# Second attention of a two-layer model: scores turned before the exponential, mask and maximum added in PSUM, division left to the last mixture

## What is computed

```python
h = h + _L1_attn_ref(_layernorm(h, axis=-1), L1_attn_Wq, L1_attn_Wk, L1_attn_Wv, L1_attn_Wo)
h = h + _L1_ffn_ref(_layernorm(h, axis=-1), L1_ffn_A, L1_ffn_B, L1_ffn_Wr, L1_ffn_br)
...
draft = jnp.einsum('bhqd,bhkd->bhqk', qr, kr)
draft = draft + jnp.where(causal_future, neg, jnp.asarray(0.0, dtype))
_, draft_indices = jax.lax.top_k(draft, num_remain)     # num_remain = 128
mask = mask.at[b_idx, h_idx, s_idx, draft_indices].set(0.0)   # all else: neg
scores = jnp.einsum('bhqd,bhkd->bhqk', qr, kr) / np.sqrt(HD).astype(np.float32) + mask
attn = jax.nn.softmax(scores, axis=-1)
out = jnp.einsum('bhqk,bhkd->bhqd', attn, v)
```

## Time and profile before

| | us |
|---|---|
| median of 3 runs (5139.87 to 5142.20) | 5141.41 |
| the profiled execution, its own time | 5140.53 |
| its span in the trace | 5138.70 |
| PE busy | 3749.4 (73%) |
| DVE busy | 3507.8 (68%) |
| ACT busy | 3167.7 (62%) |

### The profile page before, as it was taken

How to read it: one execution, slowest core, us unless ns; L and a number is a source line. 1 busy time by engine, 2 the same in 40 slices (tenths; PEclk the granted TensorE clock), 3 DMA queues, 4 the chain that set the end, 5 groups by cost and what they waited for, 6 DMA issues and landing times. The chain is left out here.

```text
span 5138.7 us, 79699 instructions
## 1 busy us (share of the span) xinstructions
PE 3749.4 (73%) x23338; PEld 2207.5 (43%) x23480; DVE 3507.8 (68%) x10383; ACT 3167.7 (62%) x7058; POOL 289.1 (6%) x213
## 2 busy tenths in 40 slices
PE   6998999999999999924555355555555555554799
PEld 2445766666444444412333233333333333332454
DVE  3564777776333356558888888888888888887444
ACT  1123777776000011169999599999999999999200
POOL 2332000000000023300000000000000000000000
PEclk8999999999999999966766676666766767766899
DMA  4235323232111123310011011111011110110222
GB/s 150 64 70 157 78 54 79 57 76 94 57 49 49 49 49 76 77 37 10 17 27 26 1 26 26 26 23 25 6 26 26 24 25 6 24 26 6 79 86 78
DMA packets 276875, 249.81 MB, mean 49 GB/s; under 512 B 170048, under 2 KB 209232, under 8 KB 276432
## 3 DMA queue, kind: packets, MB, share of 16 engines
q1 hardware_dynamic: 275888, 245.13, 18.1%
q0 software_dynamic: 544, 0.07, 0.0%
HBM read 167.56 MB, written 77.59 MB: 48 GB/s over the span
## 5 line engine op out<-in xcount | busy, mean ns | idle before, releaser
L1036 ACT ACTIVATE a_sign<-a_x,a_state 128x384 fp8e4<-128x384 f32 (+5 forms) x1536 | 1343.0, 876 | 124.4 <-DVE a_state L1172 85.7
L942 PE MATMUL a_ps_s<-k,q 128*128 128x512 bf16 (+3 forms) x1474 | 500.1, 484 | 689.5 <-DVE a_x L1273 660.0
L953 PE MATMUL a_ps_t<-ident,arena 128*128 128x128 f32 x2304 | 484.8, 355 | 193.9 <-ACT a_invT L1005 130.1
L942 PEld LDWEIGHTS a_ps_s<-k,q 128*128 128x128 bf16 x1536 | 167.4, 130 | 914.6 <-DVE a_x L1273 748.3
L971 PE MATMUL a_ps_o<-a_probT,vals 128*32 128x128 f32 x4608 | 407.4, 327 | 184.8 <-ACT a_probT L1001 184.4
L953 PEld LDWEIGHTS a_ps_t<-ident,arena 128*128 128x128 f32 x2304 | 338.4, 179 | 332.8 <-ACT a_invT L1005 142.9
L727 ACT ACTIVATE a_prob<-a_x_neg,a_shift 128x640 f32<-128x640 f32 (+7 forms) x512 | 397.1, 776 | 79.4 <-DVE a_x_neg L770 61.2
L1273 DVE TENSOR_SCALAR_CACHE_REDUCE a_x<-a_ps_s 128x128 f32<-128x128 f32 (+7 forms) x512 | 383.7, 754 | 85.4 <-PE a_ps_s L945 60.4
L1001 ACT COPY a_probT<-a_ps_t 128x512 f32<-128x512 f32 (+3 forms) x768 | 346.6, 476 | 111.1 <-PE a_ps_t L953 110.1
L770 DVE TENSOR_SCALAR_CACHE_REDUCE a_x_neg<-a_ps_s 128x640 f32<-128x640 f32 (+7 forms) x512 | 378.8, 751 | 38.4 <-PE a_ps_s L651 25.4
L971 PEld LDWEIGHTS a_ps_o<-a_probT,vals 128*32 128x32 f32 x4608 | 269.2, 128 | 294.4 <-ACT a_probT L1001 268.2
(11 more groups left out here) (229 smaller groups left out, 5941.4 us busy)
## 6 DMA issues: line engine op xcount, KB each, us to landing
q<-qk SPq DMA_DIRECT2D x256, 256.0 KB, 4.8
qk<-p_qkT SPq DMA_DIRECT2D x32, 960.0 KB, 6.2
h_rows<-h SPq DMA_DIRECT2D x32, 512.0 KB, 6.9
k<-qk SPq DMA_DIRECT2D x256, 64.0 KB, 5.1
h<-tok_h SPq DMA_DIRECT2D x16, 512.0 KB, 4.0
arena<-in_wo SPq DMA_DIRECT2D x16, 512.0 KB, 9.0
o<-a_o SPq DMA_DIRECT2D x16, 512.0 KB, 2.7
q<-o SPq DMA_DIRECT2D x16, 512.0 KB, 5.6
```

What stands on the lines that cost most here:

```text
L942: nc.tensor.matmul(ps_s[:, n % 2, a:a + w], q[:, y, head, i * P:(i + 1) * P], k[:, y, a:a + w], start=(y == 0), stop=False, skip_group_che ...
L953: mm = nc.tensor.transpose(ps_t[:, (n + 1) % 3, c:c + P], prob[:, par, at:at + P], ident[:, :])
L1036: ins = nc.scalar.activation(to, x[:, par, at:at + w], ACT.Sign, scale=-1.0, saturate=False, bias=state[:, par, 0, n:n + 1], accum_out=sta ...
```

## The change

In the second attention:
- The exponentials on ACT (16 a pair) are gone, and so is `keep`. DVE instead writes a mask for each of the 14 tiles, `mark`: 0 where the score is kept and -1e18 where not, from float32 scores to bf16, without a sum.
- PE turns the raw scores into `ps_t` and adds two things there: the negated row maximum, one matmul a chunk (L979, 24 a pair, up to 512 columns, from `topT`, three bf16 parts of 16 maxima, through `row_of`), and the turned mask, one 128x128 bf16 matmul a block (L984, 70 a pair). The evacuation by ACT is now the exponential (L1036 of the changed kernel) instead of a copy, 24 a pair.
- The values have 32 columns of ones beside them, so that the same matmul also gives the row sums: the stationary operand is 64 wide instead of 32, and `ps_o` holds two banks. `invert`, the turned inverses and their copy are gone. `output` copies 1024 columns where `normalise` multiplied 512.
- `start` splits the maxima into three bf16 parts; PE turns them once a pair (L993) and ACT copies them at the end of p = 2 (L1040).
- `ps_t` is a ring of two banks, not three. Scores lie in three buffers instead of two (two of them where `prob` was). The loop body has six slots instead of two. DVE waits at p = 2 for the turns of pair s-2 (`turn_done`) before it writes the mask, where it waited for ACT's exponentials.
- SP stores the row sums too: four transfers a pair instead of two.

In the last mixture: the sums are loaded for each row tile (four transfers), and DVE takes their reciprocal (128x1024) and multiplies (128x1024) before the tile is projected; for tile 0 it does so at p = 2 of the last slot.

```diff
@@ kept_attention, PE
                     def turn(n, m, i, a, w):
-                        if n >= 2:
-                            pe.wait_ge(probT_ready, (s - 2) * TURNED + (n - 1))
+                        to = ps_t[:, (n + 1) % 2, 0:w]
+                        pe.wait_ge(probT_ready, (s - 2) * TURNED + max(n, 1))
                         for c in range(0, w, P):
                             at = ps_seg(m, i) + a + c
-                            mm = nc.tensor.transpose(ps_t[:, (n + 1) % 3, c:c + P], prob[:, par, at:at + P], ident[:, :])
+                            nc.tensor.matmul(to[:, c:c + P], xs[old][:, at:at + P], ident[:, :], start=(c == 0), stop=False,
+                                             is_transpose=True, skip_group_check=True)
+                        mm = nc.tensor.matmul(to.rearrange("p (b c) -> p b c", c=P), row_of[:, m * TT + i, :],
+                                              topT[:, :].unsqueeze(1).to_broadcast([SPLITS * 2 * TT, w // P, P]),
+                                              start=False, stop=(i == 0), skip_group_check=True)
+                        for c in range(0, w if i else 0, P):
+                            at = ps_seg(m, i) + a + c
+                            mm = nc.tensor.matmul(to[:, c:c + P], mask[:, at:at + P], ident_b[:, :], start=False,
+                                                  stop=True, skip_group_check=True)
                         mm.then_inc(turn_done, 1)
...
-                        turn_inverse()
...
+                    if st["keep"]:
+                        turn_top()
@@ ACT
-                        nc.scalar.copy(probT[:, n % 4, 0:w], ps_t[:, (n + 1) % 3, 0:w]).then_inc(probT_ready, 1)
+                        nc.scalar.activation(probT[:, n % 4, 0:w], ps_t[:, (n + 1) % 2, 0:w], ACT.Exp).then_inc(probT_ready, 1)
...
-                            for n in EXPS[p]:
-                                exps(n, par)
+                        if p == 2 and st["keep"]:
+                            top_evac()
@@ DVE
-                        return nc.vector.scalar_tensor_tensor(out=prob[:, y, at:at + w], in0=x[:, y, at:at + w],
-                                                              scalar=limit[:, r:r + 1], in1=prob[:, y, at:at + w],
-                                                              op0=ALU.is_ge, op1=ALU.mult,
-                                                              accum_out=total[:, y, n:n + 1])
+                        return nc.vector.tensor_scalar(mask[:, at:at + w], old_x[:, at:at + w], limit[:, r:r + 1], MASKED,
+                                                       ALU.is_lt, ALU.mult)
...
-                        nc.vector.tensor_tensor(o[:, :], ps_o[:, :], invT[:, :], ALU.mult).then_inc(o_ready, 1)
+                        nc.vector.tensor_copy(o[:, :], ps_o[:, :]).then_inc(o_ready, 1)
...
-                                dve.wait_ge(exp_done, (s - 1) * (2 * TT) + 2 * TT)
+                        if p == 2 and st["value"]:
+                            dve.wait_ge(turn_done, (s - 2) * TURNED + TURNED)
...
+                        if p == 2 and isinstance(s, int) and s == PAIRS + 1:
+                            scale_first()
@@ last_mixture
+def scale(nc, dve, o, total):
+
+    nc.vector.reciprocal(total, total)
+    dve.drain()
+    return nc.vector.tensor_tensor(o, o, total, ALU.mult)
...
-                        pe.wait_ge(o_in[j % RING], landed(j))
+                        pe.wait_ge(scaled, j + 1)
...
+                scale_rows(1)
                 residual(0)
                 dve.wait_ge(rest_in, 48)
                 for j in range(NT):
+                    if j + 2 < NT:
+                        scale_rows(j + 2)
```

More of the change, by code:

```diff
@@ L521, in load_values, with store_heads @@
         wait()
-    sp.dma_start(v, v_dram[:, ds(v_at, TT * DH)]).then_inc(arrived, 16)
-def store_strips(sp, gi, y, o, o_dram, done, wait):
+    sp.dma_start(v, v_dram[:, ds(v_at, TT * DH)].rearrange("p (t d) -> p t d", d=DH)).then_inc(arrived, 16)
+def store_heads(sp, gi, y, o, o_dram, total_dram, done, wait):
     g, b = gi % HKV, gi // HKV
@@ L997, in _, with slot, top_evac @@
             def _(act):
-                def slot(s, par, st):
+                def slot(s, turn_of, st):
+                    par, mine = turn_of % 2, turn_of % 3
                     def evac(n, m, i, a, w):
                         act.wait_ge(turn_done, (s - 2) * TURNED + (n + 2))
-                        nc.scalar.copy(probT[:, n % 4, 0:w], ps_t[:, (n + 1) % 3, 0:w]).then_inc(probT_ready, 1)
-                    def inverse_evac():
-                        act.wait_ge(turn_done, (s - 2) * TURNED + 1)
-                        nc.scalar.copy(invT[:, :], ps_t[:, 0, :]).then_inc(probT_ready, 1)
+                        nc.scalar.activation(probT[:, n % 4, 0:w], ps_t[:, (n + 1) % 2, 0:w], ACT.Exp).then_inc(probT_ready, 1)
+                    def top_evac():
+                        act.wait_ge(turn_done, (s - 1) * TURNED + 1)
+                        nc.scalar.copy(topT[:, :], ps_t[0:SPLITS * 2 * TT, 0, 0:P]).then_inc(probT_ready, 1)
                     EVAC_PASSES, BETWEEN = 2, 40
@@ L1062, in slot @@
                                 evacs(p * NS + n)
-                        if st["search"] and p in EXPS:
-                            if p == 2 and st["value"]:
-                                act.wait_ge(turn_done, (s - 2) * TURNED + TURNED)
-                            for n in EXPS[p]:
-                                exps(n, par)
+                        if p == 2 and st["keep"]:
+                            top_evac()
                 over_slots(act, slot)
@@ L1306, in exact_where_needed @@
                                     if n in KEEPS[2]:
-                                        keep(n)
+                                        mark(n)
                                 dve.nop()
@@ L1333, in part @@
                             for r in keeps:
-                                keep(r).then_inc(prob_ready, 1)
+                                mark(r).then_inc(mask_ready, 1)
                             if keeps:
@@ L1351, in part @@
                                     gather(n, y)
-                        if p == 4 and st["keep"]:
-                            invert()
+                        if p == 4:
+                            dve.drain()
                         if p == 4 and st["score"]:
-                            dve.drain()
                             for n in range(NS - 4, NS):
```

179 lines of the change are left out of this document (98 added, 81 removed).

## The result

The changed kernel takes 5276.58 us (median of 4 runs, 5273.68 to 5278.96) against 5140.64 us before: a ratio of 1.0264, interval 1.0246 to 1.0282. It is slower by 136 us; 5093 was forecast, 5020 to 5190 the range. Its profiled span is 5277.1 us.

What follows compares the result with a forecast made beforehand. In the search, the loop of count, narrow, count was taken to bound p = 2, and PE ACT's copies behind p = 0. 5140.5 - 60 (30 slots) - 8 (first two) + 20 (tail) = 5092.5, so 5093; range 5020 to 5190.

Steps and rivals of the forecast that it cites:

- p = 2 to 4: Search passes: without ACT's exponentials and with cheaper marks, 1.4 + 1.0 + 2.4 = 4.8 us a slot saved.
- PE's added work: Search, p = 0 and 1: masks, wide row matmuls and changes of kind add 11 us a pair at full clock.
- p = 0 and 1: Search passes where turns are evacuated: +2.8 us a slot, bounds +1.3 at full clock and +6 at half.
- My runs: ACT's back-to-back evacuations in p = 0 and 1: the first takes 5.1 us at full clock, 8.1 at half.
- the spread copies: Evacuations outside the two runs: covered at full clock, 3.2 us of PE a pair of chunks against 3.7 us.
- The rival in which PE becomes the bound at half clock: p = 0 keeps a half-clock stretch and p = 1 gets one: value stage +6 to +9, 5186 to 5280 us; 20%.
- The first two slots: Search slots without values, where only the savings stand: 3 and 5 us, 8 in all.
- The last value stage: After the search, running alone: +11 us on 21.9 at full clock; `output` and `scale_first` behind it +2.
- The mixture: 14 tiles scaled in DVE's stream: 9.8 us of work in 8.8 idle, 0.9 us a tile, +7 us (0 to 13).

Runs made afterwards that it cites:

- h1: e4 without the 24 row matmuls a pair, masks kept (exponentials taken without the negated maximum): 4986.33 us, ratio 0.9698.
- e2: The changed kernel with totals loaded only once into each of the four buffers, later tiles scaled with old values: 5186.10 us, ratio 1.0088.
- e3: The changed kernel without the reciprocal in the last mixture, loads of totals and product kept: 5190.75 us, ratio 1.0095.
- e4: The changed kernel, nothing left out, with SP issuing row and totals loads for tile j+4 two iterations before `y_ready` of tile j: 5149.20 us, ratio 1.0017.
- e1: The changed kernel whose last mixture neither loads totals nor scales tiles 1 to 15: 5136.98 us, ratio 0.9991.

## Why the prediction was wrong, step by step

- **p = 2 to 4: right.** Forecast 1.4, 1.0 and 2.4 us less; measured 14.3 to 12.9, 14.1 to 13.0, 15.8 to 13.2 (medians; the passes were to last 12.9, 13.0 and 13.3).
- **PE's added work: 2 us a pair too low, two errors against each other.** 11 us a pair at full clock were forecast. Busy PE in p = 0 and 1 rose from 25.7 to 36.3 us, but at different clocks (0.76 and 0.82), so this is no measure of it. At full clock the masks take 0.24 us for four (3752.48 to 3752.72), 4.2 us a pair where I had 4.9; a row matmul of 512 columns with its two borders takes 0.43 us (a turn is 1.15 us with it, 0.72 without it in h1) where the columns alone take 0.22. I had the border as a change of kind at 0.1 us a chunk; it was a change of rows, at 0.1 us twice, and zeros in the other rows take it away. By these prices the rows cost 3.8 us of columns and 5.0 of borders, with the masks 13 us a pair (an estimate from the turns above).
- **p = 0 and 1: mechanism right, size off.** Forecast +2.8 us a slot (bounds 1.3 and 6), measured 38.2 - 33.8 = +4.4. My runs were 5.1 us at full clock and 8.1 at half; the first took 6.5 at full clock. I took PE to be at full clock in the spread copies ahead of it; it was at 0.54 for 15.2 us and came into the run with nothing in hand. The rival in which PE becomes the bound at half clock had this for p = 0, but its +6 to +9 also wanted such a stretch in p = 1, and there the clock was 1.00. ACT waited 5.4 us a slot for `ps_t` in p = 0 and 1.8 in p = 1, where 4 to 7 were to show. 5.1 less 4.4 leaves 0.7 us a slot, 20 us in all, and not 60. The first two slots gave 7 us (8 forecast). The stage began 4.5 us later; e2 and e3, alike up to there, began it at 2225.7 and 2225.5 as the kernel before did, so this differs from one execution to the next and is not the change's.
- **The last value stage: +14.7 us, 11 forecast.** DVE's wait is 36.64 us (33 forecast, 21.92 before). Neither stage ran at full clock, as I had taken it: the granted clock was 0.85 over this wait, with the first 10.3 us at 0.50, and 0.89 over the one before. The reciprocal and the product behind it cost nothing: from the end of DVE's copy to the first projection it is 8.3 us, before 8.4, where +2 was forecast.

```profile
4816.34 1.22 DVE L1311 COPY a_o<-a_ps_o 128x1024 f32<-128x1024 f32 x1 [36.64 <-PE a_ps_o L1003]
4817.48 6.54 DVE L546 RECIPROCAL a_first_total<-a_first_total 128x1024 f32<-128x1024 f32 x1
```

- **The mixture: the step that failed, +7 us forecast, +142 measured.** I charged 0.9 us a tile for 9.8 us of DVE's work in 8.8 us of idle time. The work was even less (6.55 + 1.23), and e4 shows that it fits. What was not in the sum at all are the transfers that feed it. The prediction counts SP's added stores in the search, and here nothing: each tile waits for four new transfers (2.6 us of issue, the last landing some 10 us later), which SP issues only after `y_ready` of the tile four back, while the first use of the buffer moved one iteration forward, from PE's projection to DVE's scaling. So issue, landing, scaling and the next `y` became one loop of 29.2 us a tile. Measured from the first projection on, 142 us: 14.3 until the first `y`, 130 in the twelve tiles behind it (10.8 each), 2 less at the end. No rival named it, so the range missed it.
- **Without that step.** e1, in which the mixture takes 309 us again, is at 5137: inside the range, but 44 us above the forecast and the same as the kernel before, not faster. So the size of the search was off as well, which is a quarter of the 184 us that the prediction missed.

## What to carry to other kernels

When a step is put ahead of another on a ring of buffers, write down for the same buffer who frees it, when its load is issued and when it is first used; the number of iterations between is the lead, and it can go to nothing while every engine has room. And before a matmul with fewer than 128 rows is put between full ones, try it with zeros in the rest.

## What the hardware did that I had not expected

- A matmul of 48 rows between ones of 128 stops the weight loads at both borders, 0.10 us each at full clock; 128 rows with 80 of zeros were 117 us faster, 3.4 us a slot.
- PE's clock fell with less work: without the 70 mask matmuls it was 0.53 in p = 0 of about every other slot and 0.65 to 0.69 in the others, with them 0.62 to 0.80. PE was busy 99% of p = 0 even in the slots at 0.53, so a busy PE alone did not bring full clock. The time of p = 0 goes with it, from 20.2 us at 0.80 to 23.5 at 0.62 in one trace, e4:

```profile
3656.67:3676.99 20.32, 19.39 (x146) 11.76 (x146) 17.66 (x49) 15.92 (x39) 0.00 (x0) 0.80 0.00 1
...
3732.81:3754.50 21.69, 21.53 (x146) 13.07 (x146) 18.45 (x50) 16.03 (x38) 0.00 (x0) 0.68 0.34 73
```

- The reciprocal takes 6.55 us for 128x1024, 6.4 ns a column, where 16 columns took 0.253; my estimate from those was 8.6.
